# W2 loaded by its first 768 columns, eight accumulators in turn, and four moved pieces in the token stage of a fused low-rank chain

## The reference

```
L0: einsum('bct,bcd->bdt', x, W0[adapter])                       # mixes the 64 tokens of a sequence
L1: x @ W1   + (x @ A1[adapter]) @ B1[adapter]                   # rank 16, 16 adapters
L2: x @ W2.T + ((x @ A2[labeler]) @ B2.T) * 0.5                  # rank 32, 5 labelers
L3: x @ W3.T + 2 * gates-weighted sum over 8 experts of (x @ A3[e].T) @ B3[e].T   # rank 16
    # logits = x @ Wr.T + 5 * onehot(language); the two largest are kept, softmax of them gives the gates
```

## Time and profile before

| | |
|---|---|
| three runs | 537.42, 537.88, 537.42 us, median 537.42 |
| profiled execution | 537.65 us, of which the span on the core is 535.9 |
| PE busy | 525.2 us, 98% of the span, 2764 matmuls |
| DVE, ACT, POOL busy | 301.3, 186.0, 170.7 us |
| TensorE clock granted | 1.00 of full speed (2.4 GHz) throughout |
| PE's waits of over 0.1 us | 7.4 us in nine waits, four in the first 34 us and five from 269 us on |

### The profile page before, as it was taken

One profiled execution on the slowest core, in us unless ns is written; L12 is line 12 of the kernel. 1 busy time (PEld: TensorE's weight loads), 2 busy tenths in 40 slices (PEclk: granted clock), 3 DMA queues, 4 the chain that ended last, 5 costly groups with the idle time before them and its releaser, 6 DMA issues.

```text
span 535.9 us, 8929 instructions
## 1 busy us (share of the span) xinstructions
PE 525.2 (98%) x2764; PEld 458.2 (86%) x2764; DVE 301.3 (56%) x635; ACT 186.0 (35%) x342; POOL 170.7 (32%) x250
## 2 busy tenths in 40 slices
PE   7999999999999999999989999999999999999996
PEld 7999999998888888888877788888888888888885
DVE  3942233289733332369888674765747647565463
ACT  4641221136122223257434323333333333233331
POOL 2501000002010212127856536443354343543400
PEclk9999999999999999999999999999999999999999
DMA  8804020013431102040611323314223242132302
GB/s 280 297 35 134 2 79 16 1 41 120 146 115 55 51 29 72 8 146 18 186 51 57 98 79 114 84 56 126 83 78 90 81 125 86 58 93 78 124 24 78
DMA packets 23246, 46.79 MB, mean 87 GB/s; under 512 B 6820, under 2 KB 11044, under 8 KB 23092
## 3 DMA queue, kind: packets, MB, share of 16 engines
q1 hardware_dynamic: 23028, 45.85, 26.1%
q0 software_dynamic: 192, 0.59, 0.3%
HBM read 33.39 MB, written 13.04 MB: 87 GB/s over the span
## 4 chain that ended last, share of the span: by engine, by line
PE 88%; POOL 3%; DVE 3%; issue 2%; DMA 1%; POOLq 1%; ACT 1%; SPq 0%; DVEq 0%; ACTq 0%
PE bank L1599 25%; PE bank L1465 16%; PE bank L1533 12%; PE bank L1588 8%; PE bank L1507 5%; PE bank L1519 5%; PE bank L1481 4%; PE bank L1647 4%; PE bank L1655 4%; PE bank L1650 1%; PE bank L1649 1%; DMA w2raw<-in_w_dram 1%; POOL em_lo L613 1%; POOL em_hi L609 1%; PE bank L1609 1%
## 5 line engine op out<-in xcount | busy, mean ns | idle before, releaser
L1599 PE MATMUL bank<-t_hi,em_hi 128*128 128x512 f32 x168 | 57.2, 403 | 0.0
L1043 DVE TENSOR_TENSOR em_lo<-bank,em_hi 128x384 fp32r<-128x384 f32 (+2 forms) x40 | 19.4, 496 | 66.0 <-ACT em_hi L745 53.0
L1043 DVE TENSOR_TENSOR w1t_lo<-raw,w1t_hi 128x1024 fp32r<-128x1024 f32 x18 | 24.2, 1345 | 23.7 <-ACT w1t_hi L775 17.1
L1599 PEld LDWEIGHTS bank<-t_hi,em_hi 128*128 128x128 f32 x168 | 31.1, 189 | 7.0
L1533 PE MATMUL bank<-te,em_hi 128*128 128x512 f32 x144 | 34.9, 395 | 0.0
L745 ACT ACTIVATE em_hi<-bank 128x384 fp32r<-128x384 f32 (+1 forms) x24 | 11.3, 498 | 64.7 <-PE bank L1465 57.1
L609 POOL CAST em_hi<-tba 128x256 fp32r x32 | 13.4, 447 | 63.1 <-PE bank L1588 57.6
L1533 PEld LDWEIGHTS bank<-te,em_hi 128*128 128x128 f32 x144 | 27.0, 188 | 6.6
L576 POOL DMA_DIRECT2D b2scr<-b2stage x3 | 1.8, 597 | 91.6 <-DVE b2stage L1043 91.6
L613 POOL TENSOR_TENSOR em_lo<-tba,em_hi 128x256 fp32r<-128x256 f32 x32 | 27.6, 883 | 2.4 <-POOL em_hi L609 1.2
L1043 DVE TENSOR_TENSOR em_hi<-tmp,em_hi 128x512 fp32r<-128x512 f32 x22 | 15.4, 699 | 20.5 <-ACT em_hi L882 11.4
(11 more groups left out here) (284 smaller groups left out, 1607.0 us busy)
## 6 DMA issues: line engine op xcount, KB each, us to landing
raw<-in_x_dram SPq DMA_DIRECT2D x16, 512.0 KB, 3.9
b1s<-b1scr SPq DMA_DIRECT2D x32, 217.5 KB, 2.7
raw<-in_b1w_dram SPq DMA_DIRECT2D x10, 512.0 KB, 3.6
out_dram<-ef SPq DMA_DIRECT2D x16, 256.0 KB, 2.0
out_dram<-ost SPq DMA_DIRECT2D x16, 256.0 KB, 2.4
w2raw<-in_w_dram SPq DMA_DIRECT2D x7, 512.0 KB, 7.8
graw<-in_w3a3wr_dram SPq DMA_DIRECT2D x4, 768.0 KB, 8.7
b1scr<-b1stage SPq DMA_DIRECT2D x12, 256.0 KB
```

What stands on the lines that cost most here:

```text
L1043: V.tensor_tensor(dst, src, f32(hi), ALU.subtract).then_inc(signal, 1)
L1599: ins = nc.tensor.matmul(to[:, :], left[a][:, k0 + k, :], m_right(right, z, k), start=(name in OPENS and n == 0), stop=(n == 3 * KH - 1), ...
```

## The change

Five things, all of order or of the size of a piece:

1. W2 comes by its first 768 columns: row block 0 in pieces of 128, 384 and 256 columns, each row block 1 to 7 as 128 x 768, and the last 256 columns of all eight row blocks in one transfer at the end (one cast, one subtraction). The blocks 6 and 7 of the diagonal lie in that last piece, so POOL's identities for them come after those of W3.
2. The output blocks of E go through eight banks in turn, and PE waits for the last piece of W2 before the seventh block (n = 6).
3. In pair 0: POOL reads the indices of block 1 (`choose(1)`) ahead of the diagonals of blocks 0 and 1. DVE makes the gates of block 0 before `xn_lo(1)`. PE starts b12 by three matmuls ahead of `narrow(1)`, and the small products of block 1 stand at other places between the wide ones.
4. The `lo` splits of t2 and t4 move from the end of pair 0 into pair 1: t2 behind the first low-rank step, t4 behind the routing. Pair 1 of DVE's list is written out for this ahead of the loop.
5. In the last pair the transpose of block 15's gated rows goes behind the first output tile.

```diff
-        W2PIECES = [(0, 0, P), (0, P, D // 2), (0, D // 2, D)] + [(k, 0, D) for k in range(1, K)]
+        FIRST = OUTER * P
+        W2PIECES = [(0, 0, P), (0, P, D // 2), (0, D // 2, FIRST)] + [(k, 0, FIRST) for k in range(1, K)]
+        W2ALL = len(W2PIECES) + 1
...
-        IDENTITIES = [("g", n) if kind else ("w", n) for n in range(K) for kind in ((0, 1) if n >= 2 * F3C // P else (0,))] \
+        IDENTITIES = [("w", n) for n in range(OUTER)] + [("g", n) for n in range(2 * F3C // P, K)] + [("w", n) for n in range(OUTER, K)] \
...
+            sp.dma_start(w2all[:, :, FIRST:], w2.rearrange("(k p) n -> p k n", p=P)[:, :, FIRST:]).then_inc(s_win[W2ALL - 1], 16)
             sp.dma_start(b2raw[:, :, :], b2).then_inc(s_b2r, 16)
...
             pool.wait_ge(s_s0l, 1)
+            chosen = choose(1)
             pool.wait_ge(s_bdz, 2)
             diagonal(0, 0, 0)
             diagonal(1, 1, 0)
-            take(1, choose(1))
+            take(1, chosen)
...
+            act.wait_ge(s_diag, DIAG["w", K - 1])
+            nc.scalar.activation(W2S[0][:, :, FIRST:], w2all[:, :, FIRST:], ACT.Copy).then_inc(s_w2h, 1)
...
+            dve.wait_ge(s_w2h, W2ALL)
+            lo(W2S[1][:, :, FIRST:], w2all[:, :, FIRST:], W2S[0][:, :, FIRST:], s_w2l)
...
                 back_sum("t4")
+                gates(0, 0, steps)
                 xn_lo(1, YB)
...
                 first_low_rank(1, 1, steps)
-                gates(0, 0, steps)
...
-                dve.wait_ge(s_tf, FORMED["t4"])
-                split_lo("t2", FRONT)
-                dve.wait_ge(s_tb, FORMED["t4"])
-                split_lo("t2", BACK)
-                split_lo("t4", FRONT)
-                split_lo("t4", BACK)
...
                 first_low_rank(b0, 0, steps)
+                if after_first:
+                    dve.wait_ge(s_tf, FORMED["t4"])
+                    split_lo("t2", FRONT)
+                    dve.wait_ge(s_tb, FORMED["t4"])
+                    split_lo("t2", BACK)
...
                 route(b0, 0, steps)
+                if after_first:
+                    split_lo("t4", FRONT)
+                    split_lo("t4", BACK)
                 sum_p1(p)
...
-                    pe.wait_ge(s_accl, n - 5)
-                    product(bank[n % 6], ob, c, range(K)).then_inc(s_acc, 1)
+                    above(pe, s_accl, n - 7)
+                    if n == OUTER:
+                        pe.wait_ge(s_w2l, W2ALL)
+                    product(bank[n % 8], ob, c, range(K)).then_inc(s_acc, 1)
...
                 h2_into(0, 0)
+                group(a21, "b12", 3, 0, 3, True)
                 narrow(1, second_block, YB)
-                group(a21, "b12", 3, 0, 8, True)
+                group(a21, "b12", 3, 3, 11, True)
                 mixed(1, 1)
-                group(a21, "b12", 3, 8, 12, True).then_inc(s_pw, 1)
-                group(a22, "b21", 2, 0, 4, False)
+                group(a21, "b12", 3, 11, 12, True).then_inc(s_pw, 1)
+                group(a22, "b21", 2, 0, 6, False)
                 h1_across(1, 1)
...
-                gated_across(b1, 1)
-                for n in range(4):
+                if not last:
+                    gated_across(b1, 1)
+                tile(p, 0, False, last)
+                if last:
+                    gated_across(b1, 1)
+                for n in range(1, 4):
                     tile(p, n, False, last)
```

32 lines of the change are left out of this document (17 added, 15 removed).

## The result

The changed kernel took 531.83 us (median of four runs, 531.3 to 532.0), beside 537.65 us for the kernel before (four runs, 537.42 to 539.53): ratio 0.9882, 95% interval 0.9859 to 0.9906. It is faster, as forecast, but by 5.8 us and not 4.5. The profiled execution took 531.3 us with a span of 529.5, against 537.65 and 535.9 before. 531.83 lies outside the range that the forecast gave to its own sum (532.2 to 533.9), on the fast side. It is still inside the wide range of 531.5 to 534.9, but one of the four runs, the profiled one, lies outside that too. Where the sum failed is told further down, term by term. One run of the kernel before, among those taken beside the experiments, took 1049.81 us and is left out everywhere.

A forecast was written before the change was run, and what follows sets the result against it. PE was taken as the bound, busy 98% of the span at full clock, with nine waits of 7.4 us. Terms 1.1 + 0.45 + 1.5 + 0.55 + 0.9 = 4.5 us gave 533.0 us, own range 532.2 to 533.9, wide 531.5 to 534.9.

The forecast's parts named there:

- k = 1: Sign in the first stage: PE starts W2's row block 1 at 9.6 to 10.2 us, against 10.93 before.
- the wait at mixed(3): Surest sign, in pair 1: a new PE wait of 1.1 to 1.5 us for DVE at mixed(3).
- W2: First stage: fewer bytes ahead of row block 1 and a shorter cast, -1.1 us (-0.2 to -1.3).
- Banks: First stage, n = 6: banks 6 and 7 are free, so PE's wait goes, -0.45 us (-0.3 to -0.5).
- Second chain: Pair 0: waits at narrow(1) (-1.24) and for the gates (-0.53) go, 0.3 charged; -1.5 us (-0.2 to -1.8).
- t2 and t4 into pair 1: Pair 1: 1.89 + 0.3 won, 0.3 charged for t2, 1.35 for mixed(3); -0.55 us (+0.2 to -1.0).
- Last gates: Last pair: tile 0 no longer awaits the transpose, 0.98 gone, 0.1 charged; -0.9 us (-0.5 to -1.0).
- The port rival: Pair 1: shared DVE/POOL port moves waits, t2's front meeting POOL's first sum, block 0's gates take(2); 534.6 us, chance 0.18.
- t4 wasn't hidden: Rival in pair 1: DVE reaches the sums early enough, mixed(3) doesn't wait, 1.35 less, 531.6 us; chance 0.08.
- the first stage did follow the size of the pieces: Denies the first-stage rival that bytes don't govern the landing and only the shorter cast counts: 533.9 us, chance 0.10.
- the last piece was 5.8 us early: Denies the rival that W2's last piece is late at n = 6: slower than before, at worst 539 us, chance 0.03.

The follow-up runs named there:

- the halves of the cut: Changed kernel with one W2 cut undone, each twice: row block 0's third piece whole, 532.6 and 532.15 us; row blocks 1 to 7 whole, 532.99 and 532.61 us.
- six banks: Changed kernel with the first stage's output blocks going through six banks in turn, as in the kernel before: 531.95 us.
- The runs of each half: Changed kernel with one edit: choose(1) again behind the wait for the diagonals, 532.39 us; or block 0's gates and PE's pair 0 order as before, 532.12 us.
- t4 behind the gates: Changed kernel with both splits of t4 moved behind block 3's first low-rank step in pair 1: 532.37 us.
- rows whole: Changed kernel with W2's row blocks 1 to 7 whole; only row block 0's third piece stays cut: 532.99 us, the second time 532.61 us.
- `xn_lo(3)` first: Changed kernel with xn_lo(3) ahead of the second left side and the second sum in pair 1: 531.6 us.
- t2 alone at the seam: Changed kernel with t2's splits back at the end of pair 0, t4's staying in pair 1: 532.35 us.
- t2 and t4 at the seam: Changed kernel with the splits of t2 and t4 both back at the end of pair 0: 532.78 us.

## Why the forecast was right in kind and short by a quarter

The places came out as the forecast said: no new wait but the one at mixed(3), no wait for the last piece of W2, diagonal(2)'s add at 0.45, no wait in pairs 2 to 6. Two of its signs missed by their size: k = 1 started at 9.27 and not at 9.6 to 10.2, and the wait at mixed(3) was 0.72 and not 1.1 to 1.5. The sum was 4.5 and the profile has 6.34. What failed are the charges for new lateness: 0.3 in the second chain, where none came, and 0.3 + 1.35 in pair 1, where 1.28 came. Term by term:

- **W2: 1.1 forecast, 1.66 in this profile, 1.3 as a mean over twelve.** The mechanism holds and its size was near; 0.36 of the excess is an early landing, which is luck. The landing of the third piece was 0.92 us sooner, not the 0.5 I gave 128 KB at 236 KB/us. The rate came from one stretch, and the halves of the cut show that bytes ahead on the queue counted for more than a row block's own. By the rule of the Trainium skill (DMA: Bandwidth & Descriptors, Anatomy of one DMA) the term would have been an estimated 0.8; the row's rate was nearer. The page fits that rule to transfers issued by GpSimd, and W2's are issued by SP, which the forecast didn't say.
- **Banks: 0.45 forecast, 0.58.** The wait at n = 6 was read right; the last 0.12 us lie behind it and go with six banks too.
- **Second chain: 1.5 forecast, 1.96.** The failed step is the charge: 0.3 us for `xn_lo(1)` and the low-rank step behind the gates. None came. The gates took 1.59 us, as the forecast had it, but they began sooner than it had them: t1's two splits took 1.75 and 0.69 us and not 2.29 and 0.94, since take(1) had moved out of their way, and `xn_lo(1)` ended at 270.45, 0.77 us before PE asked for it. The rest of the excess, 0.19 over the 1.24 + 0.53 of the two waits, isn't accounted for. The runs of each half show what I had not seen, that choice and gates overlap by 0.35.
- **b3's cast: 0 forecast, 0.22.** Not in my list at all, and not the change's doing but luck. SP issued b3 2.24 us sooner, just as much as PE was ahead. The cast began 6.14 us after the issue, and in the kernel before it had been 6.86, which held up h2T's copy. Where it was 6.85 to 6.93 with the changed kernel's order (t4 behind the gates, rows whole the second time, `xn_lo(3)` first) the same shift was between -0.06 and 0.02.
- **t2 and t4 into pair 1: 0.55 forecast, 1.07.** The 1.89 was right to the hundredth, and the wait for h1c with what followed gave 0.46 where I had 0.3. The failed step is the charges, 0.3 for t2 and 1.35 for mixed(3), which came to 0.25, 0.88 and 0.15 behind them. I had worked out mixed(3)'s lateness from a PE that is on time, so the 1.35 had t2's 0.3 in it already: measured so, mixed(3) was 1.13 late (0.25 + 0.88). The run with t2 alone at the seam shows it: nothing delays PE for t2, and mixed(3) costs 1.12. A PE that has been held up once arrives later and waits less, and I charged both in full. The port rival was right that t2's front meets POOL's first sum (2.22 us) and that the gates of block 2 are slow beside take(4) (2.67 us, 302.55 to 305.22), but PE lost only the 0.25 to the one and 0.09 to the other.
- **Last gates: 0.9 forecast, 0.98.**

With W2 at its mean the excess is 0.2 + 0.13 + 0.46 + 0.22 + 0.52 + 0.08, less the 0.13 lost over the later pairs, 1.5 us in all, and the medians say 1.3 (5.8 against 4.5). The stretch of the later pairs differs by itself from profile to profile, between 0.20 lost and 0.20 won, with no wait listed in it. Apart from the luck, the common fault is that I charged for every lateness I could name and credited none that vanished by itself. The rivals fell: t4 wasn't hidden, the port didn't move the waits, the first stage did follow the size of the pieces, and the last piece was 5.8 us early.

**And the clock.** In the profile with t2 and t4 at the seam the granted clock halved behind the 1.72 us wait at mixed(2), and its pair 1 is worth -1.20 us where the waits alone make 0. Of that kernel's four runs this one alone has a mean granted clock of 0.997, and it is the slowest. The kernel before has the same wait. Its profile shows full clock there, but of the 28 runs of it beside the experiments 7 have a mean granted clock of 0.996 or 0.997, and those take 538.07 to 539.34 us, mean 538.66, the others 536.36 to 538.18, mean 537.35. Of the 60 runs of kernels that have at least t4 in pair 1, the first six of rows whole left aside, none is under 0.999. So it may be that the removed wait is worth, in one run of four, some 1.2 or 1.3 us more than its own length. That isn't shown: where the clock of these seven runs fell isn't known, only their mean, and rows whole had two of its first six runs at 0.997 (535.28 and 534.41) without that wait, which I can't explain.

## What to carry to other kernels

Read a small gain from the shift of the same instruction in two profiles, part by part, and not from medians, when something early in the kernel lands by chance: here 1.4 us of landing scatter hid terms of 0.5 us that the shifts gave to a tenth. When work is moved off a seam into a busier stretch, compare each piece with the idle time ahead of each dependent step, and move only the pieces that fit: 0.68 us behind the second low-rank step gave 0.66 back, 2.4 us ahead of it gave nothing. Don't add charges for two latenesses of which one waits out the other. And when work moves on one engine, look at what it ran beside: here POOL's take(1), moved forward, shortened two subtractions on DVE by 0.79 us.
